# Attention and graph layers on one core: eight units with a PSUM bank each become seven units that draw on a pool of eight banks, scores matmuls alternate between three row groups, and a replay in the text sets every engine's order

## The chip, the cores and the metric

One NeuronCore of a Trainium2 chip. The time is that of one execution on the device in microseconds (us), the median of several runs. PE is TensorE (matmuls write to PSUM, eight banks of 512 fp32 columns), ACT is ScalarE, DVE is VectorE, POOL is GpSimd, SP issues DMAs.

## What is computed

64 independent batches: x of 128 x 384 (128 nodes) and adj of 128 x 128. Four layers, each followed by a residual and a layer norm:

```python
x = _layernorm(x + _L0_gnn_ref(x, adj, ...))
x = _layernorm(x + _L1_gnn_ref(x, adj, ...))
x = _layernorm(x + _L2_gnn_ref(x, adj, ...))
x = _layernorm(x + _L3_gnn_ref(x, adj, ...))
```

L0 is attention of 12 heads of 32 columns, masked by adj. L1 is two graph layers: scores h W_left h and h W_right h (upper and lower triangle), exponential times adj, mixing of a projection, an inner norm with relu. L2 is two layers with u = h h / sqrt(384), a softmax, and three projections mixed by the upper part, the diagonal and the lower part. L3 is again 12-head attention, with adj as a bias, and an output projection. In all 19 weights of 384 x 384.

## The kernel before

Everything is kept at about fp32 accuracy by pairs of fp16 numbers: a tensor is `hi + lo`, and a product is three matmuls (hi hi, hi lo, lo hi). Per batch, called a unit, PE runs 547 matmuls: eight projections `project_across` (27 matmuls of 128 columns, L563 to L565, two of them with three bias matmuls, L569), eleven `project_natural` (nine of 384 columns, L575 to L577, nine of them with a bias, L581), eight `scores` steps of nine matmuls (L630), eight `attend` steps of nine matmuls of 33 columns (L645 to L647), and the small products of L1 and L2 (L613 to L615, L652, L669, L676, L681).

A scores or attend step s holds three heads, one in each of three 128-column tiles t, all in the same 32 partitions `HD * g` (g = s % 4). So the scores matmuls contract over 32 rows, and the nine of one step are all of row group g and write three parts of one bank:

```python
head = slice(HD * g, HD * g + HD)
for t in range(DT):
    for qp, kp, n in ((a_hi, b_hi, 0), (a_hi, b_lo, 1), (a_lo, b_hi, 2)):
        last = pe.matmul(banks[u][:, t * N:(t + 1) * N], lhsT=qp[u][head, t, :], rhs=kp[u][head, t, :],
```

After a scores step DVE adds the mask and takes the minimum of each row (L760, three times an instruction and its read of the accumulator), ACT takes the exponential (L515, three times) and rounds to fp16 (L521), DVE makes the low half (L771), and SP transposes both halves by DMA (L374) into `turned` for `attend`. A projection is rounded by ACT (L506) and its low half made by DVE (L744). Between layers the input is rounded by ACT (L501), its low half made by POOL (L403) or DVE (L738), and transposed by DMA (L366).

Eight units are in flight (`UNITS = 8`). Each has its own PSUM bank, its own set of tiles and its own semaphores, so a step waits only for its own unit. Unit i + 8 loads its x when unit i has made its last residual (L357). Every engine works through a fixed list: `sequence(engine)` sorts all steps of all 64 units by `START[i] + TIMES[step]`, a table of moments written in the file, with units 44.578 us apart. Two pairs of these moments put scores steps of two units five apart side by side on PE, (4) with (1) and (6) with (2):

```python
    ("scores", 1): {PE: 24.72, SCALAR: 39.36, VECTOR: 34.22, SYNC: 45.00},
    ("scores", 2): {PE: 38.12, SCALAR: 50.97, VECTOR: 49.01, SYNC: 48.89},
    ("scores", 4): {PE: 247.38, SCALAR: 259.22, VECTOR: 255.16, SYNC: 259.63},
    ("scores", 6): {PE: 260.69, SCALAR: 275.25, VECTOR: 270.15, SYNC: 276.09},
```

5 x 44.578 is 222.89, so step 1 of unit i + 5 falls 0.23 us after step 4 of unit i. Over the whole list the 512 scores steps stand in 392 runs. The weights are loaded once, 5.2 us apart, into tiles borrowed from units 4 and up, whose work must wait (`stages_free`).

Of the kernel before, what the change touches and what calls it, by code (L numbers as in the profile page):

```python
# [5 lines left out]
F32, F16 = mybir.dt.float32, mybir.dt.float16  # L6
ACT = mybir.ActivationFunctionType
ALU = mybir.AluOpType
# [9 lines left out]
UNITS = 8  # L18
# [4 lines left out]
BANK = 512  # L23

# [16 lines left out]
PERIOD = UNITS * 44.578  # L41
TIMES = {
    ("load", 0): {SYNC: 0.06},
    ("turn", 0): {SCALAR: 2.01, POOL: 4.67, SYNC: 1.92},
    ("masks", 0): {VECTOR: 8.87},
    ("project", 2): {PE: 8.96, SCALAR: 12.16, VECTOR: 11.85},
    ("bias_x", 0): {POOL: 11.39},
    ("project", 0): {PE: 15.33, SCALAR: 16.54, VECTOR: 16.90},
    ("project", 1): {PE: 17.09, SCALAR: 21.86, VECTOR: 21.58},
    ("scores", 0): {PE: 21.20, SCALAR: 30.26, VECTOR: 28.97, SYNC: 34.18},  # L50
    ("scores", 1): {PE: 24.72, SCALAR: 39.36, VECTOR: 34.22, SYNC: 45.00},
    ("scores_lo", 0): {VECTOR: 31.47},
    ("attend", 0): {PE: 34.49, SCALAR: 39.44},
    ("scores", 2): {PE: 38.12, SCALAR: 50.97, VECTOR: 49.01, SYNC: 48.89},
    ("scores_lo", 1): {VECTOR: 41.53},
    ("attend", 1): {PE: 46.05, SCALAR: 52.77},
    ("scores", 3): {PE: 48.36, SCALAR: 58.82, VECTOR: 53.60, SYNC: 65.33},
    ("scores_lo", 2): {VECTOR: 52.85},
    ("attend", 2): {PE: 57.34, SCALAR: 61.37},
    ("scores_lo", 3): {VECTOR: 60.87},  # L60
    ("attend", 3): {PE: 63.22, SCALAR: 67.49},
    ("turn_adj", 0): {PE: 66.17, SCALAR: 72.48, POOL: 72.42},
    ("divide", 0): {VECTOR: 67.52},
    ("residual", 0): {VECTOR: 70.16, POOL: 67.62},
    ("turn", 1): {SCALAR: 78.01, POOL: 73.94, SYNC: 85.64},
    ("norm", 0): {SCALAR: 77.73},
    ("project", 3): {PE: 81.24, SCALAR: 88.70, VECTOR: 91.01},
    ("project", 4): {PE: 89.50, SCALAR: 95.94, VECTOR: 95.53},
    ("u_gcn", 0): {PE: 95.77, SCALAR: 104.15, VECTOR: 98.90},
    ("project", 5): {PE: 105.05, SCALAR: 108.95},  # L70
    ("delta_gcn", 0): {VECTOR: 105.47},
    ("mix", 0): {PE: 107.12},
    ("inner", 0): {VECTOR: 109.57, POOL: 107.47},
    ("gain", 0): {VECTOR: 114.21},
    ("turn", 2): {SCALAR: 117.22, VECTOR: 118.27, SYNC: 122.60},
    ("project", 6): {PE: 122.80, SCALAR: 127.48, VECTOR: 125.75},
    ("project", 7): {PE: 124.00, SCALAR: 132.84, VECTOR: 134.94},
    ("u_gcn", 1): {PE: 130.53, SCALAR: 141.00, VECTOR: 138.74},
    ("project", 8): {PE: 136.59, SCALAR: 143.97},
    ("minus_adj", 0): {POOL: 140.47},  # L80
    ("delta_gcn", 1): {VECTOR: 142.42},
    ("mix", 1): {PE: 144.89},
    ("inner", 1): {VECTOR: 149.00, POOL: 147.19},
    ("residual", 1): {VECTOR: 153.05, POOL: 150.20},
    ("gain", 1): {VECTOR: 152.08},
    ("turn", 3): {SCALAR: 157.16, POOL: 153.25, SYNC: 162.30},
    ("norm", 1): {SCALAR: 157.01},
    ("u_di", 0): {PE: 158.62, SCALAR: 166.32, VECTOR: 163.30},
    ("project", 9): {PE: 165.18, SCALAR: 169.05},
    ("project", 10): {PE: 168.54, SCALAR: 173.45},  # L90
    ("delta_di", 0): {VECTOR: 169.14},
    ("project", 11): {PE: 171.53, SCALAR: 178.59},
    ("turn_delta", 0): {PE: 176.95, VECTOR: 182.46},
    ("sums", 0): {POOL: 178.60},
    ("mix", 2): {PE: 179.28},
    ("inner", 2): {VECTOR: 186.03, POOL: 183.71},
    ("gain", 2): {VECTOR: 187.35},
    ("turn", 4): {SCALAR: 189.25, VECTOR: 190.13, SYNC: 197.54},
    ("u_di", 1): {PE: 195.47, SCALAR: 200.81, VECTOR: 198.13},
    ("project", 12): {PE: 198.59, SCALAR: 202.19},  # L100
    ("project", 13): {PE: 202.03, SCALAR: 206.92},
    ("project", 14): {PE: 204.53, SCALAR: 212.35},
    ("sums", 1): {POOL: 206.94},
    ("delta_di", 1): {VECTOR: 207.55},
    ("turn_delta", 1): {PE: 210.99, VECTOR: 211.29},
    ("mix", 3): {PE: 212.37},
    ("inner", 3): {VECTOR: 215.39, POOL: 223.21},
    ("gain", 3): {VECTOR: 218.82},
    ("residual", 2): {VECTOR: 221.10, POOL: 225.28},
    ("norm", 2): {SCALAR: 223.53},  # L110
    ("turn", 5): {SCALAR: 224.23, POOL: 226.26, SYNC: 224.67},
    ("project", 17): {PE: 235.25, SCALAR: 238.89, VECTOR: 241.35},
    ("bias_x", 1): {POOL: 235.72},
    ("project", 15): {PE: 241.56, SCALAR: 245.84, VECTOR: 245.78},
    ("project", 16): {PE: 245.12, SCALAR: 251.07, VECTOR: 251.43},
    ("scores", 4): {PE: 247.38, SCALAR: 259.22, VECTOR: 255.16, SYNC: 259.63},
    ("scores", 5): {PE: 257.23, SCALAR: 263.62, VECTOR: 261.46, SYNC: 268.40},
# [16 lines left out]
}  # L134


START = [2.0 + i * PERIOD / UNITS for i in range(B)]


STAGES = 3  # L140
# [782 lines left out]
```

## Time and profile before

| | us |
|---|---|
| median of 3 runs | 3090.86 |
| lowest, highest | 3088.84, 3092.55 |
| the profiled execution | 3095.68 |
| its span, first to last instruction | 3093.9 |

| engine | busy us | share of the span |
|---|---|---|
| PE, matmuls | 2961.7 | 96% |
| PE, weight loads | 2240.0 | 72% |
| DVE | 2503.8 | 81% |
| ACT | 1833.4 | 59% |
| POOL | 1129.4 | 37% |

A busy engine has at least one instruction in flight. Matmuls are pipelined, each lasting longer than the distance to the next, so for PE the busy share tells only that it did not stand still; how fast it goes is told by the distance from start to start. Views by stage give the busy time and the number of instructions in a stretch of the span; "idle before" in a view by line is the time in which the engine had nothing in flight before instructions of that line.

### The profile page before, as it was taken

Reading aid. Unit: us, or ns where it says so; the run is one execution under the profiler, and the core shown is the slowest. Engines: PE = TensorE matmul, PEld = TensorE weight load, DVE = VectorE, ACT = ScalarE, POOL = GpSimd, SP = SyncE. Lnnn points to the kernel's source line nnn. Section 1 sums busy time; section 2 is a strip of 40 time slices with the busy share of each in tenths; the row PEclk is TensorE's granted clock in tenths of the full one; section 3 lists DMA queues with packets and bytes.
Section 4 is the critical chain, followed back from the end, with each engine's and each line's share of the span. In section 5 each row is a group of like instructions: output and inputs, shape, how many; then the busy total and the mean of one; then the engine's idle time right before and its main releaser. Section 6 shows DMA issues by size and latency. Waiting matters only on the chain.

```text
span 3093.9 us, 91346 instructions
## 1 busy us (share of the span) xinstructions
PE 2961.7 (96%) x35008; PEld 2240.0 (72%) x35008; DVE 2503.8 (81%) x8824; ACT 1833.4 (59%) x4885; POOL 1129.4 (37%) x2315
## 2 busy tenths in 40 slices
PE   3799999999999999999999999999999999999985
PEld 2677777777777777777777777777777777777753
DVE  5578888888888888888888888888888888888763
ACT  5456566666566666666656656666666665666542
POOL 1233333343343333334334334333333433333321
PEclk7899999999999999999999999999999999999996
DMA  7233443444444444444444434434444434443322
GB/s 212 49 61 70 77 80 74 75 80 79 70 80 80 69 80 77 71 81 79 72 75 80 79 71 81 79 68 81 78 74 78 78 73 75 80 77 72 65 50 44
DMA packets 804111, 237.84 MB, mean 77 GB/s; under 512 B 771552, under 2 KB 803424, under 8 KB 803552
## 3 DMA queue, kind: packets, MB, share of 16 engines
q1 hardware_dynamic: 796336, 219.42, 39.4%
q10 hardware_dynamic: 7344, 12.58, 1.3%
q8 instruction: 281, 4.60, 0.6%
q14 instruction: 150, 1.23, 0.1%
HBM read 30.54 MB, written 12.58 MB: 14 GB/s over the span
## 4 chain that ended last, share of the span: by engine, by line
PE 88%; DMA 6%; DVE 2%; ACT 2%; POOL 1%; issue 1%; SPq 1%; POOLq 0%; DVEq 0%; ACTq 0%
PE bank L575 11%; PE bank L577 10%; PE bank L576 10%; PE bank L630 8%; PE bank L563 8%; PE bank L565 8%; PE bank L564 8%; PE bank L681 7%; DMA turned<-flat 5%; PE bank L581 3%; PE bank L613 3%; PE bank L676 3%; PE bank L614 2%; PE bank L615 2%; PE bank L645 1%; PE bank L647 1%
## 5 line engine op out<-in xcount | busy, mean ns | idle before, releaser
L563 PE MATMUL bank<-turned,w_hi 128*128 128x128 f16 x4608 | 821.4, 220 | 12.8 <-DVE ab L744 5.1
L565 PE MATMUL bank<-turned,w_lo 128*128 128x128 f16 x4608 | 821.8, 221 | 0.0
L564 PE MATMUL bank<-turned,w_hi 128*128 128x128 f16 x4608 | 821.8, 221 | 0.0
L506 ACT ACTIVATE ab<-bank 128x384 f16<-128x384 f32 (+1 forms) x896 | 436.6, 487 | 636.0 <-PE bank L581 240.7
L575 PE MATMUL bank<-w_hi,turned 128*128 128x384 f16 x2112 | 693.1, 328 | 25.2 <-DMA turned<-flat 23.5
L576 PE MATMUL bank<-w_lo,turned 128*128 128x384 f16 x2112 | 692.9, 328 | 0.0
L577 PE MATMUL bank<-w_hi,turned 128*128 128x384 f16 x2112 | 692.9, 328 | 0.0
L515 ACT ACTIVATE score<-score,small 128x128 f32<-128x128 f32 x1536 | 499.9, 392 | 91.0 <-DVE small L760 73.6
L744 DVE SCALAR_TENSOR_TENSOR ab<-bank,ab 128x384 f16<-128x384 f32 x512 | 276.8, 550 | 251.0 <-ACT ab L506 251.0
L563 PEld LDWEIGHTS bank<-turned,w_hi 128*128 128x128 f16 x4608 | 457.8, 99 | 29.2 <-issue 15.6
L564 PEld LDWEIGHTS bank<-turned,w_hi 128*128 128x128 f16 x4608 | 454.2, 99 | 14.4 <-issue 0.2
L565 PEld LDWEIGHTS bank<-turned,w_lo 128*128 128x128 f16 x4608 | 454.6, 99 | 0.0
L403 POOL TENSOR_TENSOR flat<-x,flat 128x384 f16<-128x384 f32 x256 | 233.2, 921 | 517.0 <-ACT flat L501 517.0
L760 DVE CUSTOM_DVE_ANT_0 score<-bank,mask 128x128 f32<-128x128 f32 x1536 | 361.0, 284 | 7.8 <-PE bank L630 7.5
L630 PEld LDWEIGHTS bank<-ab 32*128 32x128 f16 x4608 | 250.4, 93 | 134.9 <-issue 101.9
L630 PE MATMUL bank<-ab 32*128 32x128 f16 x4608 | 318.8, 217 | 28.6 <-DVE small L760 14.2
L771 DVE TENSOR_TENSOR flat<-score,flat 128x384 f16<-128x384 f32 x512 | 275.8, 548 | 44.3 <-ACT flat L521 44.0
L577 PEld LDWEIGHTS bank<-w_hi,turned 128*128 128x128 f16 x2112 | 207.4, 98 | 139.7 <-issue 4.3
L575 PEld LDWEIGHTS bank<-w_hi,turned 128*128 128x128 f16 x2112 | 206.7, 98 | 138.5 <-issue 22.2
L450 POOL TENSOR_TENSOR small<-small,numbers_in 128x1 f32<-128x1 f32 x256 | 63.9, 250 | 662.8 <-DVE small L870 662.8
L521 ACT ACTIVATE flat<-score 128x384 f16<-128x384 f32 x512 | 267.7, 523 | 48.1 <-DMA turned<-flat 9.3
L576 PEld LDWEIGHTS bank<-w_lo,turned 128*128 128x128 f16 x2112 | 207.0, 98 | 111.2 <-issue 16.9
(118 smaller groups left out, 6503.0 us busy)
## 6 DMA issues: line engine op xcount, KB each, us to landing
turned<-flat SPq DMA_TRANSPOSE x960, 2.8
x<-x_dram SPq DMA_DIRECT2D x64, 192.0 KB, 2.6
out_dram<-score SPq DMA_DIRECT2D x64, 192.0 KB, 2.2
adj<-adj_dram SPq DMA_DIRECT2D x64, 64.0 KB, 2.4
z<-w_dram ACTq DMA_DIRECT2D x6, 576.0 KB, 4.3
score<-w_dram ACTq DMA_DIRECT2D x6, 576.0 KB, 6.1
mask<-w_dram ACTq DMA_DIRECT2D x6, 576.0 KB, 4.2
rows<-rows_dram ACTq DMA_DIRECT2D x1, 1920.0 KB, 8.4
```

The source lines that it names most:

```text
L506: act.activation(dst, src, ACT.Copy, scale=scale / WSCALE).then_inc(proj_hi_done.of(i), 1)
L515: last = act.activation(score[u][:, t, :], score[u][:, t, :], ACT.Exp, bias=top[u][:, g, t:t + 1], scale=-1.0)
L563: pe.matmul(dst, lhsT=w_hi[:, w, k, cols], rhs=t_hi[u][:, k, :], start=(k == 0), stop=False)
L564: pe.matmul(dst, lhsT=w_hi[:, w, k, cols], rhs=t_lo[u][:, k, :], start=False, stop=False)
L565: last = pe.matmul(dst, lhsT=w_lo[:, w, k, cols], rhs=t_hi[u][:, k, :], start=False, stop=(k == DT - 1 and w not in BIAS_OF))
L575: pe.matmul(dst, lhsT=t_hi[u][:, k, :], rhs=w_hi[:, w, k, :], start=(k == 0), stop=False)
L576: pe.matmul(dst, lhsT=t_hi[u][:, k, :], rhs=w_lo[:, w, k, :], start=False, stop=False)
L577: last = pe.matmul(dst, lhsT=t_lo[u][:, k, :], rhs=w_hi[:, w, k, :], start=False, stop=(k == DT - 1 and w not in BIAS_OF))
L630: last = pe.matmul(banks[u][:, t * N:(t + 1) * N], lhsT=qp[u][head, t, :], rhs=kp[u][head, t, :], start=(n == 0), stop=(n == 2))
L744: dve.scalar_tensor_tensor(low_of(i % UNITS, w), src, scale / WSCALE, hi, ALU.mult, ALU.subtract)\
L760: dve.tensor_tensor_reduce(out=score[u][:, t, :], in0=banks[u][:, t * N:(t + 1) * N], in1=(mask_bias if s < HG else minus_adj)[u], scale=1 ...
L771: dve.tensor_tensor(flat[u][:, 1, :], score_at[u], flat[u][:, 0, :], ALU.subtract).then_inc(mixed_out.of(i), 1)
```

## The change

- `UNITS` is 7, and the eight banks form one pool. `plan()` gives each PE step the banks that come free first (three for a scores step, one for any other), and `bank_is_read` makes PE wait for the read that frees each of them, whichever unit holds it. A projection or product no longer waits for the step before it in its own unit's bank.
- A scores step takes its three heads from three different row groups and puts each in a bank of its own; the matmuls go round over the three, where before they went head by head. To this end the columns of the Q and K weights are permuted on the host.
- The orders of all engines come from `plan()`: every step has a wished moment, a busy time, a time to completion and its predecessors, in the table `PARTS`; the loop takes the engine that can start first and there the step of the lowest wish among those that can start.
- The low half of the probabilities of steps 4 to 7 is made by POOL (`scores` in POOL's list) and no longer by DVE.
- The weights have staging tiles of their own, and are planned 4.4 us apart; x of unit i < 7 may be loaded from 10 i us on. The column of ones for L1's sums stands behind `flat`, which the projection that is mixed now uses. Bias loads are four small DMAs into a cleared tile.

```diff
-UNITS = 8
+UNITS = 7
...
+BANKS = 8
...
+    (SCALAR, "attend", 4): (468.02, 0.200, 0.378, ((PE, "attend", 4),), ()),
+    (POOL, "scores", 4): (375.07, 0.980, 1.050, ((SCALAR, "scores", 4),), ()),
...
+def plan():
...
+    order, free = {engine: [] for engine in ready}, {engine: 0.0 for engine in ready}
+    done, holder, banks = {}, [None] * BANKS, {}
+    left = sum(map(len, ready.values())) + sum(n > 0 for n in missing.values())
+    while left:
+        freed = sorted((done.get(h, 1e9) if h else -1.0, b) for b, h in enumerate(holder))
+        best = None
+        for engine in ready:
+            if not ready[engine]:
+                continue
+            able = [max(t, free[engine], freed[BANKS_OF.get(part[1], 1) - 1][0] if engine == PE else 0.0)
+                    for _, part, _, t in ready[engine]]
+            now = min(able)
+            if best is None or now < best[0] - 1e-9:
+                best = now, engine, min(c for c, t in zip(ready[engine], able) if t <= now + 1e-9)
+        now, engine, chosen = best
+        _, part, i, _ = chosen
+        ready[engine].remove(chosen)
+        left -= 1
+        order[engine].append((part[1], part[2], i))
+        if part not in PARTS:
+            free[engine] = now + WEIGHT_COST[part[1], engine]
+            continue
+        _, busy, until, _, _ = PARTS[part]
+        free[engine] = now + busy
+        done[part, i] = end = now + until
+        if engine == PE:
+            taken = [b for _, b in freed[:BANKS_OF.get(part[1], 1)]]
+            banks[part[1], part[2], i] = taken, [holder[b] for b in taken]
+            for b in taken:
+                holder[b] = READ_BY[part[1]](part[2]), i
+        for p, later in followers[part]:
+            j = i + later
+            if j < B:
+                soonest[p, j] = max(soonest[p, j], end)
+                missing[p, j] -= 1
+                if not missing[p, j]:
+                    ready[p[0]].append((j * PERIOD + PARTS[p][0], p, j, soonest[p, j]))
+    return order, banks
...
+BANKS_OF = {"scores": DT}
...
+            def bank_is_read(i, name, k):
+
+                for holder in BANKS_AT[name, k, i][1]:
+                    if holder is None:
+                        continue
+                    (_, read_by, n), j = holder
+                    if read_by == "project":
+                        pe.wait_ge(*(proj_hi_done if READ_BY["project"](n)[0] == SCALAR else proj_lo_done).at(j, "made", n))
+                    elif read_by == "scores":
+                        pe.wait_ge(*topped.at(j, DT - 1, n))
...
-                if g == 0:
-                    pe.wait_ge(*proj_lo_done.at(i, "made", L0_K if s < HG else L3_K))
-                else:
-
-                    pe.wait_ge(*topped.at(i, DT - 1, s - 1))
-                if g > 1:
-                    pe.wait_ge(*scalar_done.at(i, "o", s - 2))
-                head = slice(HD * g, HD * g + HD)
-                for t in range(DT):
-                    for qp, kp, n in ((a_hi, b_hi, 0), (a_hi, b_lo, 1), (a_lo, b_hi, 2)):
-                        last = pe.matmul(banks[u][:, t * N:(t + 1) * N], lhsT=qp[u][head, t, :], rhs=kp[u][head, t, :],
+                for w in (L0_V, L0_Q, L0_K) if s < HG else (L3_V, L3_Q, L3_K):
+                    pe.wait_ge(*proj_lo_done.at(i, "made", w))
+                bank_is_read(i, "scores", s)
+
+                for qp, kp, n in ((a_hi, b_hi, 0), (a_hi, b_lo, 1), (a_lo, b_hi, 2)):
+                    for t in range(DT):
+                        group = (g + t) % HG
+                        head = slice(HD * group, HD * group + HD)
+                        last = pe.matmul(bank("scores", s, i, t)[:, 0:N], lhsT=qp[u][head, t, :], rhs=kp[u][head, t, :],
```

How it moves instructions, at two places.

PE, in the middle of the program. Before, two scores steps of two units (banks 2 and 7) stand together between a projection and a product:

```order
L581 MATMUL bank_4<-bias_rows,pick 128x384
L630 MATMUL bank_2<-ab 128x128 [waits scalar_done_2,topped_2]
L630 MATMUL bank_2<-ab 128x128 x8
L630 MATMUL bank_7<-ab 128x128 [waits scalar_done_7,topped_7]
L630 MATMUL bank_7<-ab 128x128 x8
L613 MATMUL bank_5<-turned,ab 128x128 [waits proj_lo_done_5]
```

With the change, the end of an attend step and the first four matmuls of a scores step (L813) of the unit in the tiles numbered 0:

```order
L826 MATMUL bank_2<-v_1,turned 128x33
L813 MATMUL bank_6<-ab_0 128x128 [waits scalar_done_4,topped_2,proj_lo_done_0]
L813 MATMUL bank_1<-ab_0 128x128
L813 MATMUL bank_4<-ab_0 128x128
L813 MATMUL bank_6<-ab_0 128x128
```

The nine matmuls go round over banks 6, 1 and 4 and are followed by an attend step, not by more scores. They wait for readers of other units (4 and 2). Over the whole list 512 scores steps stand in 510 runs, and PE's steps name 6554 semaphores to wait for, against 5264 before.

SP's queue, at its start. Before, the second unit's x comes behind two transposes of the first unit, which wait:

```order
L344 DMA mask<-w_dram 128x3x384
L350 DMA turned<-bias_dram 128x1152
L351 DMA beta<-beta_dram 128x1
L357 DMA x<-x_dram 128x384
L358 DMA adj<-adj_dram 128x128
L366 DMA_TRANSPOSE turned<-flat 128x6x128 [waits low_made_0]
L374 DMA_TRANSPOSE turned<-flat 128x6x128 [waits mixed_out_0]
L357 DMA x<-x_dram 128x384
```

With the change:

```order
L522 DMA x_0<-x_dram 128x384
L523 DMA adj_0<-adj_dram 128x128
L513 DMA w_stage_0<-w_dram 128x3x384
L550 DMA turned<-bias_dram 2x1152 [waits dve_consts]
L550 DMA turned<-bias_dram 2x1152 x3
L551 DMA beta<-beta_dram 128x1
L531 DMA_TRANSPOSE turned<-flat_0 128x6x128 [waits low_made_0]
L522 DMA x_1<-x_dram 128x384
L523 DMA adj_1<-adj_dram 128x128
L531 DMA_TRANSPOSE turned<-flat_1 128x6x128 [waits low_made_1]
L522 DMA x_2<-x_dram 128x384
```

x of the first unit is the first DMA, and the loads of all seven units stand among the first 36 instructions; before, the third load is the 15th instruction and the eighth comes far later.

## Rows read from the trace of the kernel before

**Rows 1.** The page: busy time of the engines; the granted clock in 40 slices.
```profile
PE 2961.7 (96%) x35008; PEld 2240.0 (72%) x35008; DVE 2503.8 (81%) x8824; ACT 1833.4 (59%) x4885; POOL 1129.4 (37%) x2315
...
PEclk7899999999999999999999999999999999999996
```

**Rows 2.** Timeline of SP's queue (start us, us, instruction), and lines L357 and L378.
```profile
312.15 0.58 SPq L357 DMA_DIRECT2D x<-x_dram  x1
...
L357 SPq DMA_DIRECT2D x<-x_dram x64: 569/579/1544, 2.3 to 2828.7; - x64
...
L378 SPq DMA_DIRECT2D out_dram<-score x64: 338/578/1522, 305.1 to 3091.6; - x64
```

**Rows 3.** Stages: us; PE, PEld, DVE, ACT, POOL busy us (matmuls); clock, DMA share.
```profile
0.00:154.00 154.00, 86.61 (x983) 68.59 (x983) 83.50 (x258) 71.08 (x148) 28.18 (x53) 0.79 0.51 131
154.00:2900.00 2746.00, 2735.41 (x32748) 2075.28 (x32745) 2313.66 (x8195) 1687.41 (x4544) 1052.94 (x2157) 1.00 0.42 76
2900.00:3094.00 194.00, 139.70 (x1284) 96.15 (x1281) 106.65 (x372) 74.94 (x194) 48.25 (x107) 0.83 0.24 49
...
312.15:2828.70 2516.55, 2509.30 (x30086) 1905.08 (x30085) 2126.12 (x7536) 1551.74 (x4180) 968.93 (x1980) 1.00 0.42 77
```

**Rows 4.** Lines of PE from 312.15 to 2828.70 us: busy us, mean ns, idle before.
```profile
L630 PE MATMUL bank<-ab 32*128 32x128 f16 x3960 | 267.2, 215 | 0.0
...
L645 PE MATMUL bank<-v,turned 128*128 128x33 f16 x1320 | 141.1, 179 | 2.5 <-DMA turned<-flat 2.4
...
L613 PE MATMUL bank<-turned 128*128 128x128 f16 x330 | 61.5, 221 | 4.7 <-DMA turned<-flat 4.7
```

**Rows 5.** Timeline of PE around one scores block that stands alone.
```profile
1029.69 0.33 PE L581 MATMUL bank<-bias_rows,pick 128*128 128x384 f16 x1
1029.95 0.68 PE L630 MATMUL bank<-ab 32*128 32x128 f16 x9
1030.56 0.33 PE L652 MATMUL bank<-tri,adj 128*128 128x128 f32 x1
```

**Rows 6.** Timeline of PE: first of nine 33-column matmuls, next step.
```profile
1000.95 0.18 PE L645 MATMUL bank<-v,turned 128*128 128x33 f16 x1
...
1001.18 0.32 PE L575 MATMUL bank<-w_hi,turned 128*128 128x384 f16 x1
1001.34 0.32 PE L576 MATMUL bank<-w_lo,turned 128*128 128x384 f16 x1
```

**Rows 7.** Timeline of PE: scores steps 6 and 2 together; steps 4 and 1 together.
```profile
1005.87 1.18 PE L630 MATMUL bank<-ab 32*128 32x128 f16 x18
...
1034.17 0.98 PE L630 MATMUL bank<-ab 32*128 32x128 f16 x18
```

**Rows 8.** Lines of DVE and POOL from 312.15 to 2828.70 us.
```profile
L760 DVE CUSTOM_DVE_ANT_0 score<-bank,mask 128x128 f32<-128x128 f32 x1320 | 310.1, 284 | 0.1
L771 DVE TENSOR_TENSOR flat<-score,flat 128x384 f16<-128x384 f32 x440 | 236.4, 548 | 17.2 <-ACT flat L521 17.1
...
L760 DVE DVE_READ_ACCUMULATOR2_ANT small<- 128x1 f32 x1320 | 108.4, 82 | 0.0
...
L403 POOL TENSOR_TENSOR flat<-x,flat 128x384 f16<-128x384 f32 x220 | 199.0, 915 | 405.1 <-ACT flat L501 405.1
```

**Rows 9.** Timeline: second and eighth load of x; PE's first matmul.
```profile
34.10 0.58 SPq L357 DMA_DIRECT2D x<-x_dram  x1
...
266.40 0.58 SPq L357 DMA_DIRECT2D x<-x_dram  x1
...
16.80 0.48 PE L575 MATMUL bank<-w_hi,turned 128*128 128x384 f16 x1 [16.80 <-DMA turned<-flat]
```

**Rows 10.** Lines of ACT from 0 to 154 us.
```profile
L515 ACT ACTIVATE score<-score,small 128x128 f32<-128x128 f32 x45 | 14.7, 390 | 8.1 <-DVE small L760 8.1
...
L469 ACT ACTIVATE w_hi<-mask 128x1152 f16<-128x1152 f32 x7 | 8.1, 1161 | 6.7 <-DMA mask<-w_dram 6.7
...
L521 ACT ACTIVATE flat<-score 128x384 f16<-128x384 f32 x15 | 7.8, 523 | 5.8 <-DMA turned<-flat 4.9
```

More of the change, by code:

```diff
@@ L142 @@
 PLACE = {w: n for n, w in enumerate(WEIGHT_ORDER)}
[L143 to L159 removed]
+WEIGHTS_FROM, WEIGHT_EVERY, LOAD_EVERY = 5.5, 4.4, 10.0
@@ L162, with first @@
+BANKS_OF = {"scores": DT}
+WEIGHT_COST = {("weight", SCALAR): 1.1, ("weight", VECTOR): 1.3, ("biases", SCALAR): 1.1, ("biases", VECTOR): 2.2}
+ORDER, BANKS_AT = plan()
+def sequence(engine):
+    return ORDER[engine]
+def first(engine, name, *numbers):
+    return next((k, i) for n, k, i in sequence(engine) if n == name and (not numbers or k in numbers))
 class Signal:
@@ L186, in per_unit @@
         def per_unit(name, shape, dt=F32):
-            whole = sb(name, [shape[0], UNITS * shape[1]], dt)
-            return whole, [whole[:, u * shape[1]:(u + 1) * shape[1]] for u in range(UNITS)]
+            return [sb(f"{name}_{u}", shape, dt)[:, :] for u in range(UNITS)]
         def sem(name):
@@ L406, in bias_x, with scores @@
                 u = i % UNITS
-                if i == 0 and k == 0:
+                if (k, i) == first(POOL, "bias_x"):
                     pool.wait_ge(rows_loaded, 16)
                 pool.tensor_tensor(x[u], x[u], rows[:, X_BIAS[k], :], ALU.add).then_inc(low_made.of(i), 1)
+            def scores(i, s):
+                u = i % UNITS
+                pool.wait_ge(*cast.at(i, "p", s))
+                pool.tensor_tensor(flat[u][:, 1, :], score_at[u], flat[u][:, 0, :], ALU.subtract).then_inc(low_made.of(i), 1)
             def turn_adj(i, k):
@@ L662, in u_di @@
                 pe.wait_ge(*landed.at(i, "x", 3 + layer))
-                product(side[u], t_hi[u], t_lo[u], t_hi[u], t_lo[u]).then_inc(multiplied.of(i), 1)
+                bank_is_read(i, "u_di", layer)
+                product(bank("u_di", layer, i)[:, 0:N], t_hi[u], t_lo[u], t_hi[u], t_lo[u]).then_inc(multiplied.of(i), 1)
             def turn_delta(i, layer):
@@ L755, in scores @@
                 if g:
-                    dve.wait_ge(*mixed_out.at(i, "low p", s - 1))
+                    dve.wait_ge(*(mixed_out.at(i, "low p", s - 1) if s < HG else low_made.at(i, "p", s - 1)))
                 dve.wait_ge(*attending.at(i, "scored", s))
                 for t in range(DT):
-                    dve.tensor_tensor_reduce(out=score[u][:, t, :], in0=banks[u][:, t * N:(t + 1) * N],
+                    dve.tensor_tensor_reduce(out=score[u][:, t, :], in0=bank("scores", s, i, t)[:, 0:N],
                                              in1=(mask_bias if s < HG else minus_adj)[u], scale=1.0, scalar=BIG,
@@ L805, in u_di @@
                 dve.wait_ge(*multiplied.at(i, "u_di", layer))
-                dve.tensor_reduce(col(u, TOP), side[u], AX.X, ALU.max).then_inc(numbers.of(i), 1)
+                dve.tensor_reduce(col(u, TOP), bank("u_di", layer, i)[:, 0:N], AX.X, ALU.max).then_inc(numbers.of(i), 1)
                 dve.wait_ge(*numbers.at(i, "top of u", layer))
@@ L898 @@
     biases += [a["L3_gnn_bv"]]
+    skewed = _np.array([(HG * t + (group - t) % HG) * HD + c for t in range(DT) for group in range(HG) for c in range(HD)])
+    for w in (L0_Q, L0_K, L3_Q, L3_K):
+        ws[w] = ws[w][:, skewed]
+    for b in (BIAS_OF[L0_Q], BIAS_OF[L0_K]):
+        biases[b] = biases[b][skewed]
     rows = []
```

525 lines of the change are left out of this document (319 added, 206 removed).

## The prediction

> **What bounds the kernel now.** I read the page first. TensorE (PE) is busy for 96% of the span, and its granted clock is full except in the first two and the last of forty slices [rows 1]. A busy PE need not be a fast one, so the second view is the table by stage: from the ninth load of x (312.15 us) to the last (2828.7 us) [rows 2] lie 55 units, 2516.55 us, hence 45.76 us a unit, at clock 1.00 [rows 3]. In that stretch the scores line counts 3960 matmuls, which is 55 times 72, so the stretch holds 55 whole units, and the only idle time of PE in it is 2.5 and 4.7 us, both for transposes by DMA [rows 4]. That is 0.13 us a unit. DVE has 2126.12 / 55 = 38.7 us of work a unit, ACT 28.2, POOL 17.6 [rows 3]: the next engine has 15% of room. So a unit lasts as long as its matmuls, and time is to be had only there, or at the two ends.
>
> The ends: a unit has 35008 / 64 = 547 matmuls [rows 1]. The first 154 us hold 983 of them, worth 983 / 547 x 45.76 = 82 us of full-speed work, so 72 us are lost. The last 194 us hold 1284, worth 107 us, so 87 us are lost [rows 3]. With 64 x 45.76 = 2929 us this makes 3088, and 6 us are lost between; the span is 3094.
>
> **Scores, before.** A block of nine 32-row matmuls that stands alone: the last matmul of the projection starts at 1029.69 and streams 0.16 us (the distance of the long matmuls in [rows 6]), so the next could start at 1029.85; the block starts at 1029.95, and what follows it at 1030.56 [rows 5]. The block costs 0.71 us: 0.10 to enter, eight distances of 0.057, and 0.15 from its last start to the next step's, where 0.056 would do. About 0.19 is the price of going from full-height to 32-row matmuls and back. Eighteen in a row, from two units, show what the change is after. Where both blocks are of one row group (heads' steps 6 and 2) they last 1.18 us, where the groups differ (steps 4 and 1) 0.98 [rows 7]: matmuls in different row groups and banks already run side by side. With the same edges these pairs cost 1.21 and 1.01 us. The order before has per unit four blocks alone, one pair of each kind: 4 x 0.71 + 1.21 + 1.01 = 5.06 us. The rest of a unit is 45.76 - 0.13 - 5.06 = 40.57 us.
>
> **Scores, after.** Three row groups take turns within each block, but 510 of 512 blocks stand alone (392 runs before), so the edges are paid eight times. No row of before has this pattern. If the groups overlap fully, the nine need three rounds of 0.057 with a small shift: 0.10 + 0.13 + 0.15 = 0.38 us. If nothing overlaps it is 0.71. Between them lies how fast PE can be fed with pairs of weight load and matmul: short 33-column matmuls start every 0.026 us [rows 6], eight of which are 0.20, so 0.10 + 0.20 + 0.15 = 0.45. I take 0.45, because it is the fastest feeding that rows show over a whole block: 8 x 0.45 = 3.60 us, 1.46 us a unit less, 93 us in all. The edges added by the finer order (118 runs more, 0.19 each, 22 us) are inside this.
> The Trainium skill ("TensorE: Matmul & The Clock Gate", Part 3, The mechanism) says that matmuls of different row groups start some 4 ns apart; by that the block would come to the 0.38 of the full overlap and the sum 36 us lower, which is a rival below. The same page (Part 1, on the 56 ns) puts a floor of about 25 ns between starts, and the rows of 33 columns agree with that.
>
> **Bank pool and seven units.** A step no longer waits for its own unit's bank but for whichever of eight comes free, and a scores step for three. The order lists 6554 awaited semaphores at PE's steps against 5264, 20 more a unit. Each costs nothing as long as PE's instructions are issued ahead of it; if each took one 0.026 us start, it would be 0.5 us a unit (33 us). The nearest rows are the 0.0 idle before the scores and long matmuls [rows 4], so nothing, and 0.5 is for the range. What can really hold PE is a bank read late. A unit now has 7 x 44.4 = 311 us from load to load where it had 8 x 45.8 = 366, so less slack for DMA. I put the stalls at 0.25 us a unit, double today's, and keep 0 and 1.3 as ends.
>
> **DVE to POOL.** Four subtractions a unit, 0.55 us each on DVE, become four of 0.92 on POOL [rows 8]. DVE falls to 38.7 - 2.2 = 36.5 us, 82% of 44.4; POOL rises to 17.6 + 3.7 = 21.3, 48%. Each of four heads gets 0.37 us longer in its own chain, 1.5 us of some 311. That hides behind six other units; if PE waited for it at every head it would be 4 x 0.37 x 64 = 95 us, but POOL has half its time free.
>
> **Start.** Before, x arrives at 34.10 us for the second unit and at 266.40 for the eighth, and PE's first matmul is at 16.80 [rows 9]. After, the DMA queue puts the seven loads among its first 36 instructions. What can fill PE then? Until all seven have their first attention, ACT must do 7 x 4 heads x (3 x 0.33 + 0.52) = 42 us, 19 weight casts of 1.16 = 22 us [rows 10], and about five half-microsecond passes a unit, 17 us: some 80 us after the start. The PE work of that is, per unit, three projections (9 long matmuls at 0.16 and 60 short at 0.056, 4.8 us), 4 x 0.45 and 4 x 0.23, 7.5 us; seven give 53 us, with part of the next layer on top. So PE loses about 15 us before its first matmul and a third of the 80 after it: 42, and a little for the low clock, 45 us in place of 72. If the pool fills no better than before it stays 72; 35 is the other end.
>
> **Tail.** The last unit's load is at 2828.7 and its store at 3091.6 [rows 2], 263 us for one unit, most of it its own chain, during which PE has only 179 us of work left. With seven in flight the work left is an eighth less, and the chain gets shorter by the lighter queues alone. I take 72 us lost for 87; ends 60 and 90.
>
> **Sum.** 40.57 + 3.60 + 0.25 = 44.42 us a unit; x 64 = 2843; + 45 + 72 = 2960 us of span. The profiled execution took 3095.68 us at a span of 3093.9, and the median of the runs is 3090.86, 4.8 below it. So 2960 + 1.8 - 4.8 = **2957 us**, 4.3% less.
>
> **The rivals.**
> *Full overlap:* three streams at once, 0.38 a block, 36 us less, and ends 10 us better: 2911 us. For it: two groups do overlap in the pair. Against: no row has more than one start in 0.026 us over a whole block. 0.16.
> *Queues out of step:* the planned order meets other durations than it was planned with; a late transpose or a bank stops PE, in order, with all seven units behind it. At 1.2 us a unit beyond my stalls: 3034 us. For it: one unit less, 20 waits more. Against: 7.2 us of waits in 55 units under a fixed order too. 0.14.
> *The change doesn't do what it says:* the row groups don't overlap within a block, each stays at 0.71, + 133 us: 3090 us, no change. The 0.98 against 1.18 speaks against it. 0.04.
> *PE waits for banks (slower):* a scores step takes three of eight banks, and each is free only when DVE has read it, 3 x (310.1 + 108.4) / 1320 = 0.95 us for a step [rows 8]. If a scores step waits at PE for one such read, everything behind it on PE waits too. The gain is used up from 134 / 512 = 0.26 us a step; at every second step a full 0.95, + 243 us: 3200 us. For it: before, no unit could hold another's bank. Against: PE comes first in need and DVE has 18% of room. 0.06.
>
> **How the numbers follow.** My forecast gets 0.60. The range takes in full overlap and the out-of-step queues: 2895 to 3035, with 0.1 outside it. Faster by over 0.2% (6 us, about what a measurement of this kernel can tell from no change): forecast, full overlap and queues out of step, 0.90. Within 0.2%: most of the case without overlap, 0.03. Slower: the banks and the rest, 0.07.
>
> **What would show it.** Scores blocks of nine should last some 0.42 us to their end instead of 0.68, and never stand as eighteen. PE busy should stay over 99% in mid-run, a unit take 44.4 us there, with 547 matmuls each. The second to seventh load of x should come before 100 us. PE idle before scores on a DVE read of over 0.26 us a step would prove me wrong in sign; blocks still 0.68 us long would leave no gain but that of the ends; a unit at 44.4 with a start as before would put me 27 us low.

## The result, and the profile after

The changed kernel takes **2935.91 us** (median of 4 runs, 2934.25 to 2938.05), against 3090.15 us for the kernel before on the same chip (4 runs, 3088.84 to 3092.55): ratio 0.950, 95% interval 0.9484 to 0.9517. The forecast was 2957 us. The profiled execution took 2937.27 us at a span of 2935.5.

The page of the changed kernel, its engines and its granted clock, against [rows 1]:

```profile
PE 2824.7 (96%) x35008; PEld 2091.3 (71%) x35008; DVE 2286.8 (78%) x8566; ACT 1858.1 (63%) x4885; POOL 1336.6 (46%) x2571
...
PEclk8899999999999999999999999999999999999997
```

As many matmuls as before, 137 us less of PE time, and PE's share still 96%: PE is still the bound, and what it does takes less time. The stages, in the columns of [rows 3]:

```profile
0.00:154.00 154.00, 102.68 (x1345) 79.39 (x1346) 107.49 (x336) 84.97 (x195) 43.17 (x67) 0.87 0.57 141
250.75:2710.90 2460.15, 2449.42 (x30666) 1820.73 (x30664) 1963.69 (x7447) 1609.21 (x4256) 1164.85 (x2244) 1.00 0.46 80
500.00:2500.00 2000.00, 1990.17 (x24919) 1478.44 (x24918) 1598.74 (x6070) 1307.72 (x3460) 948.16 (x1827) 1.00 0.46 80
2742.00:2936.00 194.00, 149.77 (x1662) 102.90 (x1660) 122.97 (x449) 94.11 (x248) 77.62 (x152) 0.90 0.32 60
```

From the eighth load of x (250.75) to the last (2710.90) lie 56 units: 2460.15 / 56 = **43.93 us a unit** where it was 45.76, and 1.83 x 64 = 117 of the 158 us by which the span is shorter. The third row, 2000 us of mid-run, is the one that every experiment below is read in: 24919 matmuls / 547 = 45.56 units.

The ends give the other 41 us. The first 154 us hold 1345 matmuls (983 before), worth 108 us at the new pace, so 46 are lost in place of 72. The last 194 hold 1662 (1284), worth 133.5, so 60.5 are lost in place of 87. Between them 17.5 are lost. The loads of x and the first matmul, against [rows 9] and [rows 2]:

```profile
12.26 0.56 SPq L522 DMA_DIRECT2D x<-x_dram  x1
...
86.27 0.58 SPq L522 DMA_DIRECT2D x<-x_dram  x1
250.75 0.35 SPq L522 DMA_DIRECT2D x<-x_dram  x1
...
L543 SPq DMA_DIRECT2D out_dram<-score x64: 337/579/1720, 254.3 to 2933.1; - x64
...
13.88 0.48 PE L776 MATMUL bank<-w_hi,turned 128*128 128x384 f16 x1 [13.88 <-DMA turned<-flat]
```

Seven units are loaded by 86.27 us, where the second of the kernel before came at 34.10 and the eighth at 266.40. The last unit takes 222 us from load to store, 263 before.

Now the block of scores. PE's timeline around one that stands alone, as in [rows 5] (start us, us, instruction):

```profile
1021.81 0.33 PE L782 MATMUL bank<-bias_rows,pick 128*128 128x384 f16 x1
1022.07 0.34 PE L813 MATMUL bank<-ab 32*128 32x128 f16 x9
1022.35 0.34 PE L776 MATMUL bank<-w_hi,turned 128*128 128x384 f16 x1
```

The block is 0.34 us long (0.68 before). The long matmul ahead of it streams 0.16, so it could start at 1021.97 and starts 0.10 later. The lines of PE over the 56 units (busy us, mean ns, idle before), against [rows 4]:

```profile
L764 PE MATMUL bank<-turned,w_hi 128*128 128x128 f16 x4037 | 712.9, 220 | 7.8 <-DMA turned<-flat 7.6
...
L776 PE MATMUL bank<-w_hi,turned 128*128 128x384 f16 x1854 | 604.9, 326 | 0.4 <-DMA turned<-flat 0.4
...
L813 PE MATMUL bank<-ab 32*128 32x128 f16 x4023 | 153.3, 218 | 0.0
L824 PE MATMUL bank<-v,turned 128*128 128x33 f16 x1341 | 149.8, 180 | 1.3 <-DMA turned<-flat 1.2
...
L798 PE MATMUL bank<-turned 128*128 128x128 f16 x336 | 62.0, 219 | 1.2 <-DMA turned<-flat 0.8
```

4023 matmuls are 447 blocks, busy 153.3 / 447 = 0.343 us each, of which the last matmul takes 0.214. So from first to last start a block takes 0.129 us: nine matmuls within the time of a little over two of the distances of 0.057 that lay between any two before. The starts of one block, read singly from the trace (from 1010.288 us), are 0, 0.003, 0.007 | 0.066, 0.070, 0.073 | 0.122, 0.126, 0.128 us: three rounds, as far apart as matmuls of one row group, with three matmuls in each. Over 364 blocks from 500 to 2500 us the mean is 0.10 to enter, 0.129 within and 0.15 to leave, so the block costs **0.37 us**, where I had taken 0.45 and called 0.38 the full overlap. The Trainium skill ("TensorE: Matmul & The Clock Gate", Part 3, The mechanism) has matmuls of different row groups start some 4 ns apart; this trace agrees, with 2 to 4 ns in the block above. Its floor of 25 ns between starts (Part 1) would make eight distances 0.20, so between row groups it doesn't hold.

PE is idle 7.8 + 0.4 + 1.3 + 1.2 = 10.7 us in 56 units, 0.19 a unit, and each time for a transpose by DMA: never for a bank. What a wait costs is more than its idle time, because a long matmul is in flight for 0.33 us and the next could start after 0.16:

```profile
2045.57 0.33 PE L782 MATMUL bank<-bias_rows,pick 128*128 128x384 f16 x1
2046.40 0.23 PE L764 MATMUL bank<-turned,w_hi 128*128 128x128 f16 x1 [0.50 <-DMA turned<-flat]
```

PE stands idle for 0.50 here, but starts 0.67 late. If each distance from start to start is compared with the usual one of the same pair of shapes, PE is late by 0.34 us a unit from 500 to 2500 us, and by 0.17 in the kernel before.

### The profile page after: what moved, and what is told of

The parts are those of the page before. It is cut to its first block, busy times and chain, and to the rows that moved or that the text cites. A ratio compares the mean times of both kernels' runs of the same rounds, so it can differ in the third digit from the quotient of the medians.

```text
span 2935.5 us, 93395 instructions
## 1 busy us (share of the span) xinstructions
PE 2824.7 (96%) x35008; PEld 2091.3 (71%) x35008; DVE 2286.8 (78%) x8566; ACT 1858.1 (63%) x4885; POOL 1336.6 (46%) x2571
## 4 chain that ended last, share of the span: by engine, by line
PE 84%; DMA 7%; DVE 6%; ACT 1%; issue 1%; POOL 1%; SPq 1%; DVEq 0%; POOLq 0%; ACTq 0%
PE bank L776 11%; PE bank L777 10%; PE bank L778 10%; PE bank L764 9%; PE bank L765 8%; PE bank L766 8%; PE bank L868 7%; DMA turned<-flat 6%; PE bank L813 4%; PE bank L782 3%; PE bank L861 3%; PE bank L798 2%; PE bank L799 2%; PE bank L800 2%; PE bank L824 1%
## 5 line engine op out<-in xcount | busy, mean ns | idle before, releaser
L682 ACT ACTIVATE ab<-bank 128x384 f16<-128x384 f32 (+1 forms) x768 | 373.8, 487 | 304.3 <-PE bank L766 190.2
L586 POOL TENSOR_TENSOR flat<-score,flat 128x384 f16<-128x384 f32 x256 | 234.5, 916 | 575.9 <-ACT flat L697 575.7
L575 POOL TENSOR_TENSOR flat<-x,flat 128x384 f16<-128x384 f32 x256 | 255.6, 998 | 193.0 <-ACT flat L677 185.4
L1010 DVE BATCH_NORM_STATS2 small<-bank 128x6 f32<-128x384 f32 x256 | 144.2, 563 | 178.3 <-PE bank L861 151.5
L824 PE MATMUL bank<-v,turned 128*128 128x33 f16 x1536 | 171.8, 180 | 41.2 <-DMA turned<-flat 41.1
L868 PE MATMUL bank<-ab,score 128*128 128x384 f32 x512 | 195.8, 505 | 2.1 <-DVE score L1004 2.1
```

The source lines that it names most:

```text
L682: act.activation(dst, src, ACT.Copy, scale=scale / WSCALE).then_inc(proj_hi_done.of(i), 1)
L868: last = pe.matmul(made[:, 0:D], lhsT=delta3[u][:, m, :], rhs=proj[u][m], start=(m == 0), stop=(m == 2))
```

## The experiments

Each ratio is to the kernel before, timed on the same chip in the same job, with its 95% interval. A "unit" is 2000 us over (matmuls between 500 and 2500 us / 547).

### Row groups taken away, order kept

The theory: the time comes from row groups working side by side, and finer order, pool and seven units are only what makes room for it. The rival: the new order and the fuller ends bring a good part of it.

```diff
-                        group = (g + t) % HG
+                        group = g
```

The weight columns on the host are laid to suit; every engine's order stays word for word.

> The changed kernel (2936 us) with the three heads of a scores step in one row group again (each still in its own bank, same order of all engines, columns of Q and K not permuted). Theory, PE sets the time and the alternation of row groups is what pays: a block's starts spread over 0.46 us again instead of 0.13, so 0.34 us x 512 = 174 us more, 3110 us, slower than the kernel before, since the order now has 510 runs of scores where it had 392 and no overlapping pair. Rival, the new order and the bank pool gave the gain and PE had waits to hide longer blocks in: under 2980 us.

Measured: 3083.38 us, ratio 0.9976 (0.9966 to 0.9986). Timeline of PE, and mid-run:

```profile
1000.89 0.67 PE L813 MATMUL bank<-ab 32*128 32x128 f16 x9
1001.50 0.19 PE L824 MATMUL bank<-v,turned 128*128 128x33 f16 x1
...
500.00:2500.00 2000.00, 1996.88 (x23634) 1516.77 (x23632) 1520.18 (x5738) 1236.09 (x3284) 896.79 (x1725) 1.00 0.43 76
```

The block is 0.67 long again, 0.46 from first start to last (0.67 less 0.21 for one), and a unit 46.29 us. So the row groups are worth 147 of the 154 us, at an unchanged order. Everything else together nets 7: its ends are as short as the change's, worth some 41, but its units are 0.53 us longer than before, 34 in all. That 0.53 can be read: 118 more runs of scores, 1.84 a unit at 0.19, are 0.35, and the pair whose two groups overlapped (1.18 against 0.98, [rows 7]) is lost, 0.20. I had expected 3110 from the edges without counting that PE's stalls shrink when PE is slower: idle is 3.1 us in this stretch (9.8 in the change), and PE is late by 0.15 us a unit in place of 0.34, worth 12 us over 64 units.

### Heads one after the other within a block

```diff
-                for qp, kp, n in ((a_hi, b_hi, 0), (a_hi, b_lo, 1), (a_lo, b_hi, 2)):
-                    for t in range(DT):
...
+                for t in range(DT):
...
+                    for qp, kp, n in ((a_hi, b_hi, 0), (a_hi, b_lo, 1), (a_lo, b_hi, 2)):
```

(t outermost, so PE gets three matmuls of one row group, then three of the next.) If only neighbours in issue overlap, the block goes most of the way back.

> The changed kernel with the loops of a scores step turned: three matmuls of one head, then three of the next, the heads still in three row groups and banks. If PE looks ahead far enough over the queue, the order inside the block is nothing and the time stays 2936 us within 6. If it looks ahead only some matmuls, as in the pair of the kernel before, where the second group began after six of the first nine, blocks last between 0.45 and 0.65 us: 40 to 140 us more, 2975 to 3075.

Measured: 2947.30 us, 0.9535 (0.9520 to 0.9549). The line of scores from 500 to 2500 us, 363 blocks, and one of them:

```profile
L813 PE MATMUL bank<-ab 32*128 32x128 f16 x3267 | 129.3, 217 | 0.0
...
1007.82 0.36 PE L813 MATMUL bank<-ab 32*128 32x128 f16 x9
1008.11 0.19 PE L824 MATMUL bank<-v,turned 128*128 128x33 f16 x1
```

Blocks take 0.142 from first to last start against 0.129 in the same stretch of the change, and a unit 44.04. Turn-taking within the block is worth some 11 us; what matters is that three groups are there. The starts of this block, read singly, are 0, 0.010, 0.020 | 0.066, 0.077, 0.086 | 0.122, 0.133, 0.142: three rounds again, though three matmuls of one group stand first in the list. The trace doesn't say which record is which matmul. But with the starts in list order, six distances within one group would already make 6 x 0.057 = 0.34. So a matmul starts ahead of earlier ones of another row group, and the issue order of the nine is nearly free.

### The low halves back on DVE

```diff
-    (POOL, "scores", 4): (375.07, 0.980, 1.050, ...
+    (VECTOR, "scores_lo", 4): (375.07, 0.470, 0.630, ...
```

(for all four; the orders are planned anew, PE's comes out the same in mid-run.)

> The changed kernel with the low half of the probabilities of steps 4 to 7 made by DVE again (planned anew with that). Theory, only PE bounds: DVE rises by 2.2 us a unit from 35 to some 37.3 us of 43.9, still 85%, PE idle stays under 0.5 us a unit and the time within 10 us of 2936. Rival, DVE is the next bound and late bank reads stop PE: 30 us or more slower.

Measured: 2942.52 us, 0.9520 (0.9505 to 0.9534). Mid-run:

```profile
500.00:2500.00 2000.00, 1989.50 (x24899) 1477.33 (x24896) 1707.88 (x6246) 1306.61 (x3458) 786.77 (x1645) 1.00 0.47 80
```

DVE has 1707.88 / 45.52 = 37.5 us a unit (35.1 in the change), POOL 3.5 less, and a unit takes 43.94. Moving the four subtractions is worth some 6 us, about the bound of what can be told.

### Fewer edges: two scores steps in one block

```diff
-BANKS_OF = {"scores": DT}
+BANKS_OF = {"scores": HG}
...
-                last = pe.matmul(bank("scores", s, i, t)[:, 0:N], ...
+                last = pe.matmul(bank("scores", s, i, group)[:, half * N:(half + 1) * N], ...
```

Two steps of one unit, 18 matmuls over four banks; the orders planned anew.

> The changed kernel with two scores steps of a unit in one block of 18 matmuls, over four banks, one for each row group; a bank that holds two heads is read twice before it is free. Theory, the edges (0.10 to enter, 0.09 to leave) are paid per block: 256 of them fewer, 0.19 us each, 49 us less, and the 18 spread over some 0.32 us: 2885 us. Rival, four banks held through two reads of DVE (some 5 us apart) starve the pool and PE waits: 2936 or more, with PE idle of over 0.8 us a unit before projections or scores on a read by DVE or ACT.

Measured: 3071.06 us, 0.9935 (0.9914 to 0.9955). PE's timeline, mid-run, and what PE waits for from 500 to 2500 us (in total, times, longest):

```profile
1007.83 0.51 PE L810 MATMUL bank<-ab 32*128 32x128 f16 x18
1008.27 0.23 PE L794 MATMUL bank<-turned,ab 128*128 128x128 f16 x1
...
500.00:2500.00 2000.00, 1899.65 (x23833) 1401.62 (x23831) 1641.07 (x5801) 1232.40 (x3318) 894.99 (x1742) 1.00 0.46 76
...
PE bank L760 <- DVE ab L926: 40.5, 37, 2.0
PE bank L760 <- ACT ab L678: 14.2, 31, 0.8
```

The block itself does what was hoped: 18 matmuls until the next step in 0.44 us, where two of nine take 2 x 0.28 and one more entry of 0.10. But PE is idle for 100 us of 2000. The planner had to give another order (under half of PE's neighbours are as in the change), so this run can't say whether blocks or order cost it; the two-step block in the change's own order wasn't run. Part of the loss stands in the plan: by the busy times and moments of its own table, `plan()` leaves PE idle for 60 us from 500 to 2500, and for none in the change.

### What the ends are worth

I first tried loads 38 us apart in the plan, as the early units stood before:

```diff
-LOAD_EVERY = 5.5, 4.4, 10.0
+LOAD_EVERY = 5.5, 4.4, 38.0
```

> The changed kernel with x of the first seven units wished 38 us apart in SP's list (10 us in the change), about the distance of the kernel before. Theory, the early loads fill PE's start: the first 154 us lose some 70 us of PE work again in place of 46, the time per unit in mid-run stays 43.9 us, 2955 to 2965 in all. Rival, the early loads only bring forward what the end would have hidden: within 8 us of 2936.

Measured: 3204.36 us, 1.0358 (1.0342 to 1.0373), a unit of 47.87. That can't be a start: the plan had changed for the whole run. In its lists the change's orders repeat exactly from unit to unit; this plan's repeat for only 24% of PE's steps, and 35% of PE's neighbours are as in the change. So I looked for a spacing at which the plan comes back to the change's repeating pattern, and 30.5 does:

```diff
-LOAD_EVERY = 5.5, 4.4, 10.0
+LOAD_EVERY = 5.5, 4.4, 30.5
```

> The changed kernel with x of the first seven units wished 30.5 us apart, a value with which the planner comes back to the same repeating pattern in mid-run. Theory, only the start loses: PE's loss in the first 154 us goes from 46 toward the 72 of the kernel before, unit time 43.9 us: 2945 to 2965. Rival, late loads spoil the whole run: over 3100.

Measured: 2955.26 us, 0.9558 (0.9544 to 0.9572). Windows:

```profile
0.00:154.00 154.00, 86.86 (x1022) 67.10 (x1023) 94.87 (x279) 73.17 (x157) 33.47 (x60) 0.80 0.48 128
...
500.00:2500.00 2000.00, 1989.50 (x24934) 1479.50 (x24933) 1595.72 (x6056) 1310.72 (x3466) 945.31 (x1821) 1.00 0.46 80
```

A unit is 43.88 us, as in the change, and the first 154 us hold 1022 matmuls: 72 us lost, just what the kernel before loses. Early loads are worth 19 us of the whole: 26 at the start, of which 7 come back further on.

And the other side of it, one microsecond more:

```diff
-LOAD_EVERY = 5.5, 4.4, 10.0
+LOAD_EVERY = 5.5, 4.4, 11.0
```

> The changed kernel with x of the first seven units wished 11 us apart where it has 10, planned anew. By the written lists this one microsecond at the start throws the whole program out: in mid-run 35% of PE's neighbours are those of the change, and the pattern no longer repeats from unit to unit. Theory, the time hangs on the repeating pattern, for which the table of wishes was fitted: 3150 to 3230 us, like the run with 38 us. Rival, that run was slow for its late loads: about 2940.

Measured: 3181.27 us, 1.0292 (1.0275 to 1.0309). PE's waits from 500 to 2500 us:

```profile
PE bank L824 <- DMA turned<-flat: 74.2, 28, 3.4
PE bank L868 <- DVE score L1004: 21.1, 21, 1.2
PE bank L861 <- DVE score L986: 19.9, 21, 1.0
```

One microsecond more between loads leaves another order behind for all 64 units (24% of it repeats), which costs 245 us. The row groups and the blocks are as in the change. Much of the loss stands in the plan: by its own table it leaves PE idle for 100 us of these 2000 (the change's none), and 123 are measured. The clock adds to it. Each of the waits of 3.4 us is followed by a stretch at 1.2 GHz, 106 us in all from 500 to 2500, where the change has none; by half of that, some 53 us, PE falls behind.

### Six units, six banks

Two replanned kernels ask for the share of the seventh unit and of the pool:

```diff
-UNITS = 7
+UNITS = 6
```

> The changed kernel with six units in flight, planned anew. A unit may then stay 6 x 43.9 = 263 us from load to load; the last unit, with little beside it, took 224 us from load to end. Theory, seven units leave slack and six still leave some: PE idle rises but it stays the bound, 2940 to 3010. Rival, units already stay as long as their own chain needs, some 300 us: a unit every 50 us, 3200 or more.

Measured: 3217.72 us, 1.0404 (1.0376 to 1.0432).

```diff
-BANKS = 8
+BANKS = 6
```

> The changed kernel with a pool of six banks in place of eight, planned anew. If the pool of eight is nearly used up, as the run with four banks for a block of two steps (1.9 us of PE idle a unit more, 3071 us) suggests, six banks stop PE by 2 us a unit or more: 3060 or slower. If that run was slow because its banks were held through two reads 5 us apart, and not for their number, six cost under 0.5 us a unit: under 2970.

Measured: 3212.78 us, 1.0380 (1.0359 to 1.0401). Both carry the same flaw: 12% and 22% of PE's neighbours are as in the change, neither plan repeats (12% and 24%), and by their own tables they leave PE idle for 153 and 149 us of the 2000. They show that the planner finds nothing good there, not what a unit or a bank is worth. For the banks a cleaner test exists: the change's orders as fixed lists, and from PE's 600th step on only six banks dealt out to them (to every step, without the exception that the expectation names).

```diff
+FEW = 6
...
-ORDER, BANKS_AT = plan()
+BANKS_AT = with_banks(ORDER)
```

> The changed kernel with its own orders on all engines, word for word, but from PE's 600th step on only six banks in the pool (a few steps that could not start otherwise still take the other two). The run with six banks planned anew took 3213 us, but its order had nothing left of the change's. If number of banks is what stopped it, PE waits here too: 3100 or more. If it was the order, PE idle stays under 0.6 us a unit and the time under 2965.

Measured: 3132.72 us, 1.0127 (1.0112 to 1.0142). Mid-run and PE's waits there:

```profile
500.00:2500.00 2000.00, 1892.88 (x23042) 1403.65 (x23039) 1481.36 (x5606) 1203.09 (x3200) 873.83 (x1685) 0.98 0.41 74
...
PE bank L810 <- DVE small L991: 39.9, 39, 1.2
PE bank L859 <- ACT z L748: 36.6, 39, 1.2
PE bank L822 <- DVE score L1067: 14.5, 39, 0.4
...
708.75 0.35 PE L859 MATMUL bank<-ab 32*128 32x128 f16 x9 [0.93 <-ACT z L748]
710.11 0.22 PE L810 MATMUL bank<-turned,w_hi 128*128 128x128 f16 x1 [1.02 <-DVE small L991]
...
710.22 0.22 PE L812 MATMUL bank<-turned,w_lo 128*128 128x128 f16 x1
710.28 0.26 PE L810 MATMUL bank<-turned,w_hi 128*128 128x128 f16 x1
...
710.54 0.31 PE L810 MATMUL bank<-turned,w_hi 128*128 128x128 f16 x1
710.65 0.31 PE L811 MATMUL bank<-turned,w_hi 128*128 128x128 f16 x1
```

The kernel file has 46 lines more here: L859 is the scores block, L810 and L822 are projections. So once in nearly every unit a scores block waits for a bank that ACT is still copying for `attend` (L748), and the projection behind it waits for a bank that DVE is still reading for scores (L991), each some 1 us; idle PE is 107 us in 2000. With eight banks there are no such waits. These waits also cost clock. In the rows above, two of them are followed by a fall from 2.4 to 1.2 GHz at 710.3 us: the distance between starts goes from 0.06 to 0.11 us. From 500 to 2500 us 85 us are spent at the lower level (granted clock 0.98, against 1.00 in the change), worth some 43 us of PE time beside the idle 107. Two banks fewer cost 197 us at the same order, more than the whole change brings.

### Scores steps next to each other

Can the 0.19 of the edges be had back? First by a planner that keeps to scores while it can:

```diff
-                best = now, engine, min(c for c, t in zip(ready[engine], able) if t <= now + 1e-9)
+                best = now, engine, min((c for c, t in zip(ready[engine], able) if t <= now + 1e-9),
+                                        key=lambda c: (c[0] - (KEEP if engine == PE and c[1][1] == "scores" == last else 0.0), c))
```

> The changed kernel with one rule more in the planner: after a scores step PE takes another scores step that is ready, if its wish is not more than 20 us later than that of the first in line. The list then has 393 runs of scores where it had 510. Theory, the edges cost 0.19 us each wherever they stand: 117 fewer, 22 us less, 2914 us. Rival, DVE gets two blocks of three banks to read at once and PE waits for banks after them: 2936 or more.

Measured: 3094.78 us, 1.0003 (0.9993 to 1.0013), a unit of 46.47. It has 393 runs of scores in place of 510, and PE waits 52.5 us in 2000 for one DVE result (22 times, up to 2.5 us); 24% of the order repeats. Again the order is another one. So the second try leaves all orders as they are and only moves a scores step up by two places where just two steps lie between it and the one before (61 places, which leaves 449 runs; the banks are dealt out anew to the fixed lists):

```diff
+            steps[n + 1:n + 4] = [d, steps[n + 1], steps[n + 2]]
```

> The changed kernel with all orders kept but one move: where two steps stand between two scores steps on PE, the second scores step goes up next to the first; 449 runs of scores where the change has 510. If an edge costs 0.19 us wherever it stands and the order is otherwise kept, 61 x 0.19 = 12 us less, 2924. If moving a step early makes PE wait for three banks more, 2936 or more; if the planner's whole order was what the earlier run with 393 runs (3095 us) lost, this one must not be far from 2936.

Measured: 2946.45 us, 0.9528 (0.9514 to 0.9542): some 10 us slower than the change, where I expected 12 faster. PE's timeline at such a place:

```profile
521.21 0.34 PE L870 MATMUL bank<-ab 32*128 32x128 f16 x9
521.71 0.35 PE L870 MATMUL bank<-ab 32*128 32x128 f16 x9 [0.16 <-ACT z L759]
521.98 0.59 PE L925 MATMUL bank<-ab,score 128*128 128x384 f32 x1
```

(`d` is the scores step.) The second block starts 0.50 us after the first, 0.37 after its last start: one of its banks is still being read by ACT. At all 45 such places from 500 to 2500 us the gap is 0.37. Side by side would save 0.19; where 0.06 would do, the wait costs 0.31. The two steps that stood between were the cover of that read. That the many separate blocks are the price of three banks a block out of eight is my reading of it; another dealing of the banks wasn't run.

## Why the prediction was right

Term by term, as it was summed:

| term, us | forecast | measured |
|---|---|---|
| scores, a unit | 8 x 0.45 = 3.60 | 8 x 0.37 = 2.96 |
| stalls, a unit | 0.25 | 0.40 (what is left over) |
| the rest, a unit | 40.57 | 40.57 (taken over) |
| a unit | 44.42 | 43.93 |
| start lost | 45 | 46 |
| tail lost | 72 | 60.5 |
| between | 0 | 17.5 |
| span | 2960 | 2935.5 |

**The block** was the mis-sized term: 0.08 us a block, 8 x 0.08 x 64 = 41 us. I took the shortest start distance of 33-column matmuls, 0.026, as how fast PE can be fed. That is a distance between matmuls of one height that share the array; between row groups it says nothing. The "full overlap" I had given 0.16 is what happened, though its 2911 us didn't come, since other terms went the other way. The bounds, 0.38 and 0.71, had the answer at their edge, and the lower one should have had more weight: the pair of [rows 7] showed that groups overlap, and the 33-column rows are all of full height. The 4 ns of the Trainium skill ("TensorE: Matmul & The Clock Gate", Part 3, The mechanism) gave the better value here.

**Stalls**: idle rows rose only from 0.13 to 0.19 a unit, and 43.93 - 40.57 - 2.96 - 0.19 leaves 0.21 that shows in none. Most of it is the part of each wait that lies under a long matmul still in flight: counted from start to start, PE is late by 0.34 a unit. It was 0.17 before, so the term doubled as I had said, but from a reading that was 0.04 too small. Some 0.1 stays unexplained. The 20 extra awaited semaphores a unit aren't the cause: the usual distance from a long matmul into a scores block is 0.258 us in both kernels, and out of the block into a 33-column matmul 0.146 in both. 0.15 x 64 = 10 us over.

**Ends**: 124 us against 117. The start was right, and the run with later loads shows it is the loads that do it. The tail was 11 us better than forecast and the stretch between them 17.5 worse; I had put that at nothing, though before it was 6.

So -41 +10 +7 makes the 24 us between 2960 and 2935.5. The mechanism was right and the sum was partly lucky: with the block at its true 0.37 and the rest as forecast it would have come to 2916, 20 us too low where it was 21 too high.

**DVE to POOL**: forecast 36.5 and 21.3 us a unit, measured 35.1 and 20.8, and worth some 6 us, nearly hidden as said. **Order and pool**: forecast as nothing, as the cover was there. The run with six banks prices that cover: 197 us. My slower rival had the right size of a wait (1 us against 0.95) but not the place: it is a projection that waits for a bank DVE reads for scores, and the scores step waits for one that ACT reads for `attend`. It also left out what the clock loses behind such waits. It stays away by two banks. **Queues out of step**: not in the change. The run with loads 11 us apart shows such waits, and took 3181 us, more than the 3034 that I gave the rival, but for another reason: the danger lay mostly in the planned order itself, which by its own table has 100 of the 123 us of idle PE, and only for the rest in how the chip's durations differ from the plan's.

Left open: what a seventh unit is worth (no plan with six repeats), what a good order for six banks or for double blocks would give, and whether row groups alone, in the order and with the bank per unit of the kernel before, would have brought as much.

## What to carry to other kernels

Where matmuls use a quarter of the array's rows, issue at least three row groups to three banks close together: nine take the time of three, the order among them hardly matters, and an unchanged program around them showed it. Count what such a block holds: it takes several banks at once, so the pool and the steps that hide the readers of those banks decide whether the gain is kept. And when an order comes from a greedy planner, compare kernels at the same order; otherwise a change of one input measures the planner (245 us here) and not the input. The plan itself warns: its own idle time of PE from 500 to 2500 us is 0 for the change and for the two replanned orders that stayed fast (low halves on DVE, loads 30.5 us apart), and 60 to 153 us for the six that came out slow. Count waits from start to start, and look at the clock behind them: with six banks, two waits of some 1 us close together were enough for it to fall.

## What the runs showed of the hardware

**Entering and leaving 32-row matmuls** costs 0.10 and 0.09 us over plain distances, in the kernel before and the changed one alike, with one row group or three (from a long matmul to the block 0.258 us where 0.163 is plain, and from the block to the next step 0.146 where 0.056 is). The Trainium skill ("TensorEngine Tiling (Array Packing)", Key Properties) says that a switch of mode drains the array; the delay at both switches agrees with that, and the trace puts 0.19 us on the pair of them.

**A DVE instruction of one column can take 0.9 us.** In the kernel before, one and the same line, alone and with a subtraction on POOL beside it:

```profile
1022.96 0.15 DVE L844 SCALAR_TENSOR_TENSOR small<-small 128x1 f32<-128x1 f32 x1
...
1030.15 0.91 POOL L403 TENSOR_TENSOR flat<-x,flat 128x384 f16<-128x384 f32 x1 [2.04 <-ACT flat L501]
1030.17 0.90 DVE L844 SCALAR_TENSOR_TENSOR small<-small 128x1 f32<-128x1 f32 x1
```

It ends within 0.01 us of POOL's (1031.07 and 1031.06). In the kernel before this happens 57 times out of 128, each time with DVE starting 0.020 to 0.029 us after POOL; in the four overlaps where DVE starts earlier than that it takes 0.15. The Trainium skill ("SBUF — State Buffer", Who interferes with whom) has the two engines share a pair of ports under an exclusive lock; this agrees, and shows that the width of the DVE instruction is no protection. In the changed kernel's order the line (L1029) is never held up; durations are min/median/max in ns, of 128 each, before and after:

```profile
L844 DVE SCALAR_TENSOR_TENSOR small<-small x128: 146/151/907, 93.6 to 2976.3; 128x1 f32<-128x1 f32 x128
```

```profile
L1029 DVE SCALAR_TENSOR_TENSOR small<-small x128: 148/152/157, 106.9 to 2837.8; 128x1 f32<-128x1 f32 x128
```

A unit's two such instructions take 0.31 us in place of 1.04, which is half of the 1.4 us a unit that DVE has less to do than forecast, though POOL is busier than before.
